# A convolution block with dynamic routing: the loop over samples written out on every engine

## The reference, cut to what matters

```python
x_proj = jnp.einsum('bchw,oc->bohw', x, proj_w)                       # 128 -> 64 channels
att1 = _route(x_proj, att1_w, att1_b, [3x3, 5x5 depthwise], 1)        # one of two kernels per sample
att2 = _route(att1, att2_w, att2_b, [7x7, 9x9, 11x11 depthwise], 3)   # one of three, dilation 3
out = jnp.concatenate([att1, att2], axis=1)
att = jnp.concatenate([out.mean(axis=1, keepdims=True), out.max(axis=1, keepdims=True)], axis=1)
att = jax.nn.sigmoid(conv7x7(att, sp_w) + sp_b)                       # two maps
gate = att[:, 0:1] + att[:, 1:2]
return out * gate + x
```

## Time and profile before

| | us |
|---|---|
| median of 3 runs | 6338.1 (6338.06 to 6348.23) |
| profiled execution, its own time | 6353.46 |
| its span | 6351.9 |
| PE busy | 4896.8 |
| DVE busy | 3135.5 |
| ACT busy | 2832.8 |
| POOL busy | 1256.7 |

### The profile page before, as it was taken

One profiled execution on the slowest core, in us unless ns is written; L12 is line 12 of the kernel. 1 busy time (PEld: TensorE's weight loads), 2 busy tenths in 40 slices (PEclk: granted clock), 3 DMA queues, 4 the chain that ended last, 5 costly groups with the idle time before them and its releaser, 6 DMA issues.

```text
span 6351.9 us, 164601 instructions
## 1 busy us (share of the span) xinstructions
PE 4896.8 (77%) x62816; PEld 3336.1 (53%) x62816; DVE 3135.5 (49%) x3835; ACT 2832.8 (45%) x5378; POOL 1256.7 (20%) x2010
## 2 busy tenths in 40 slices
PE   5678897887878788787878888787887878885453
PEld 2236464655646465564745556464555646464342
DVE  3215445464545545464554545546544554645344
ACT  3455464544545455444544545354454535452120
POOL 2001011212112121211212121121212212121332
PEclk9889898898989889798988889898798979887675
DMA  9656758869697785968779696886969688696857
GB/s 225 182 133 188 174 160 217 228 182 237 191 229 198 215 223 179 227 212 217 210 194 231 180 230 207 214 227 172 233 181 242 199 217 234 179 224 156 226 131 189
DMA packets 1015814, 1285.33 MB, mean 202 GB/s; under 512 B 670750, under 2 KB 865737, under 8 KB 984414
## 3 DMA queue, kind: packets, MB, share of 16 engines
q1 hardware_dynamic: 855500, 578.24, 39.1%
q0 software_dynamic: 90800, 555.20, 28.2%
q10 hardware_dynamic: 69026, 146.11, 8.3%
HBM read 950.16 MB, written 456.70 MB: 221 GB/s over the span
## 4 chain that ended last, share of the span: by engine, by line
PE 36%; DMA 33%; DVE 11%; issue 10%; ACT 3%; POOL 2%; SPq 2%; ACTq 1%; POOLq 0%; DVEq 0%
DMA out_dram<-RX 15%; PE psC L984 13%; DMA RX<-in_x_dram 8%; DVE MM L1198 7%; DMA RX<-w_d 5%; PE psA L922 5%; PE psA L923 5%; PE psA L858 5%; PE psB L953 3%; PE psB L867 2%; DMA RX<-nat_d 2%; PE psB L932 2%; PE psB L963 2%; DVE RX L1274 1%; DVE L L1255 1%
## 5 line engine op out<-in xcount | busy, mean ns | idle before, releaser
L984 PE MATMUL psC<-RX 61*60 61x96 f32 (+7 forms) x49152 | 1457.6, 266 | 231.6 <-POOL RX L591 96.2
L984 PEld LDWEIGHTS psC<-RX 61*60 61x60 f32 x49152 | 1391.2, 132 | 304.3 <-issue 300.1
L1198 DVE TENSOR_REDUCE MM<-L 124x135 f32<-124x6480 f32 (+3 forms) x128 | 527.6, 4194 | 587.4 <-ACT L L775 587.4
L775 ACT ACTIVATE L<-psC 124x120 f32 (+4 forms) x2048 | 393.8, 284 | 830.0 <-PE psC L984 791.2
L858 PE MATMUL psA<-RX,projt 128*64 128x512 f32 x1920 | 577.0, 686 | 236.2 <-DMA RX<-in_x_dram 162.2
L922 PE MATMUL psA<-X,RX 128*128 128x240 f32 x1280 | 642.1, 591 | 125.4 <-ACT RX L740 125.3
L953 PE MATMUL psB<-ident,L 124*128 124x124 f32 x2160 | 445.5, 356 | 347.5 <-DVE RX L1274 286.6
L591 POOL COPY RX<-RX 64x720 f32<-64x720 f32 x512 | 402.3, 792 | 1455.4 <-DMA RX<-w_d 1454.4
L745 ACT ACTIVATE X<-psA,bias 128x246 f32<-128x246 f32 x1024 | 638.4, 737 | 62.6 <-PE psA L923 46.2
L923 PE MATMUL psA<-X,RX 128*128 128x240 f32 x1280 | 632.5, 583 | 0.0
L734 ACT ACTIVATE RX<-RX 32x640 f32<-32x640 f32 x320 | 233.8, 735 | 880.7 <-PE psA L923 749.9
(11 more groups left out here) (117 smaller groups left out, 5150.9 us busy)
## 6 DMA issues: line engine op xcount, KB each, us to landing
RX<-in_x_dram POOLq DMA_DIRECT2D x64, 2560.0 KB, 11.4
RX<-w_d ACTq DMA_DIRECT2D x512, 180.0 KB, 4.4
RX<-in_x_dram SPq DMA_DIRECT2D x128, 720.0 KB, 10.6
out_dram<-RX SPq DMA_DIRECT2D x128, 720.0 KB, 14.4
nat_d<-X SPq DMA_DIRECT2D x320, 280.0 KB
RX<-nat_d POOLq DMA_DIRECT2D x208, 400.0 KB, 6.8
RX<-in_x_dram POOLq DMA_DIRECT2D x416, 200.0 KB, 5.8
out_dram<-RX POOLq DMA_DIRECT2D x416, 200.0 KB, 4.9
```

The lines of the kernel that those rows point to most:

```text
L775: ins = nc.scalar.activation(dst[:, 0:NU2 - par, 15 * r:15 * r + nq, par, :], src[:, par:BR:2, :, :], ACT.Identity)
L984: ins = nc.tensor.matmul(o[:, :, 0:kk, a:b], w2t[2 * q + p][rows, ch, z:z + PB], src[rows, 2 * p + ch, 0:nf, 3 * cg + dc:3 * cg + dc + kk, ...
L1198: nc.vector.tensor_reduce(dst[0:124, mm, :].rearrange("p (f b k) -> p f b k", f=9, k=3)[:, :, par:BR:2, :], src[:, :, 0:NU2 - par, :, par, ...
```

## The change

`samples` is changed and nothing else. All 18 turns are written out, on all five engines, each with its own copy of the turn's program. The loops inside a turn stay (`repeat` for the second convolution on PE, ACT and POOL).

```diff
         def samples(eng, body):
 
-            for s in range(4):
-                body(Turn(s))
-            with eng.Fori(4, B - 1) as s:
-                body(Turn(s))
-            for s in range(B - 1, B + 2):
+            for s in range(B + 2):
                 body(Turn(s))
```

## The result

The changed kernel takes 6274.6 us (median of 4 runs, 6264.4 to 6293.3) against 6343.2 for the kernel before on the same chip: a ratio of 0.9895, 95% interval 0.9866 to 0.9924, or 69 us less by the medians, between 48 and 85 by the interval. The forecast was 6272 us, 66 us less. Its profiled execution took 6264.4 us with a span of 6262.4.

The account below looks back on a forecast made before the run. No single engine bounds the kernel; each stage of a turn has its own last wait. Savings of 34 + 4 + 21 + 7 = 66 us, with added code at 0, took 6338.1 to 6272 us, range 6236 to 6316.

Parts of the forecast that it names:

- Step 1: Second convolution's end to projection's end: without ten branches POOL's gap before loading x block 2 goes, 3.4 us each, 34 us.
- Step 2: Routing: DVE's 30 dependent steps no longer wait for counts computed in the loop, 0.36 us a turn, 4 us.
- Step 3: First convolution with f2 and f1: looped turns come down by turn 3's 1.9 us each, 21 us.
- if the first convolution's mean doesn't move: Sign against the forecast, which expected the first convolution at 181 us on average in the profile after.
- Rival A: Whole kernel: only branches and routing count, both convolutions' differences are transfer scatter; 23 us less, 6315 us; chance 0.20.
- Step 4: Second convolution: its inner loop stays, so only a few register instructions go, 0.6 us a turn, 7 us.
- Step 5: Added code: written and looped turns run through the same straight stretches and fetch them alike; set at 0.
- rival C: Projection, f2, f1: written-out code is fetched too late for PE; two missed fetches a turn give 6353 us; chance 0.04.

Follow-up runs that it names:

- e9: Kernel before with two turns in each pass of its loop (turns 4 to 13) and turn 14 written out, on every engine; 6303.2 us, 0.9952.
- e1: Kernel before with only POOL's turns 4 to 14 written out, the other engines keeping the loop; 6292.2 us, 0.9940.
- e2: Kernel before with only PE's turns 4 to 14 written out, the other engines keeping the loop; 6314.8 us, 0.9971.
- e8: Kernel before, run unchanged for a second profile; 6324.7 us, 1.0001.
- e4: Kernel before with its loop replaced by eleven loops of one pass, whose counts were folded into constants; 6254.2 us, 0.9877.
- e6: Kernel before, loop kept on every engine, with the load of x block 2 moved ahead of the stores of map 1; 6249.5 us, 0.9891.
- e5: Changed kernel with the load of x block 2 moved ahead of the stores of map 1; 6194.9 us, 0.9793 of the kernel before.
- e7: e5 with PE turning the maps after the projection's ninth step instead of the sixth; 6126.9 us, 0.9675 of the kernel before.
- e10: e7 with the passes of the second convolution written out too; 6371.6 us, 1.0060 of the kernel before.
- e11: Changed kernel with the passes of the second convolution written out too on PE, ACT and POOL; 6499.5 us, 1.0264 of the kernel before.

## Why the prediction was right, step by step

- Step 1, branch and projection, 34 us: right in size and in cause. 3.3 us for each branch in e9, 10 branches, 33 us; POOL's 3.5 us, not PE's 3.7, is on the path (e1 against e2). One detail was wrong: what hides PE's branch is DVE's work ahead of the maps, more than the wait for block 2. Turn 3's own 64.3 us of projection, which the sum left aside, was scatter: it takes 65.4 in e8 and 66.5 in the changed kernel.
- Step 2, routing, 4 us: measured 15.64 to 15.43, 2.3 us. My reason, DVE's counts, was wrong: e2 leaves DVE in its loop and has 15.46, e1 leaves PE in it and has 15.63. It is PE's written code that shortens this stage; by which instruction stays open.
- Step 3, first convolution, 21 us: not shown. The first pair of profiles moved by 2.3 us a turn, as forecast, but the second profile of the kernel before (e8) lies at the changed kernel's value, and by the prediction's own sign ("if the first convolution's mean doesn't move") this step fails. Rival A was right on this point.
- Step 4, second convolution, 7 us: too small. 13 us come from PE's register instructions in its inner loop; the first pair of profiles shows 2.1 us a turn, 23 us.
- Step 5, code fetched in the straight part, 0: right in the sum, wrong in its reason. The queue carries less (193 packets against 218), and PE starts each turn without idle. But "fetch them alike" is not so: the "issue" stops in the second group went from 20.5 to 45.0 us, and the stage shows no cost only as PE's waits for POOL shrank by about as much. Against rival C stood that turns 0 to 3 and 15 show no such stop; turn 3 has one of 2.04 us and turn 2 one of 3.04, in the second convolution and not in the stages that C named.

The sum came out right (66 against 69) by luck in part: step 3 was put too high and step 4 too low. What the runs show, 33 + 2 + 13, is 48 us, the lower end of the measured 48 to 85; e4, nearly the same program, gave 56 to 99. Some 20 us are therefore not assigned. The first convolution averages 181.3 us over the four kernels that loop on every engine (before, e8, e6, e9) and 179.9 over the six written out on all (after, e4, e5, e7, e10, e11), which would be 15 of them, but e8 against the first profile shows that single means differ by more than that. The granted clock of this stage differs too, 0.816 on average in those four and 0.824 in those six; whether it is a cause or goes along is not shown. This stays open.

The Trainium skill's "Runtime: NRT & Kernel Launch", section "Instruction fetch mechanics", also says that kernels prefer full unrolling. For the outer loop the runs agree, with 69 us; for the inner one the measurement decides against it, 225 us slower. The Trainium skill's remark in the same section that the fetch hides behind the issue of instructions does not hold on PE in the second convolution: the changed kernel loses 45.0 us to "issue" in the second group of turns 4 to 14, and e11, where the stage is written out, stands 317 us by "issue" in all, the changed kernel 100.

## What to carry to other kernels

A loop's branch costs what the engine behind it makes late, not what that engine itself stands idle: find which engine's first act after the branch is waited for, and move that act ahead of whatever holds it, which here gave as much with the loop still in place (e6, 75 us by the medians) as removing the loop (69). Write out a long outer loop, and leave a short inner loop with back-to-back small matmuls as a loop: before writing it out, compare the bytes of its code with its time (here three packets of 16.4 KB in 11.0 us, where they came 4.9 us apart). Before sharing a gain out over stages, profile the same kernel twice; a difference between two kinds of turn inside one execution (e9) tells more than two profiles.

## What the runs showed of the hardware

- A taken branch over a turn's code costs 3.3 to 3.9 us on PE, about 6.3 on SP and about 2.8 on POOL. The branch instruction itself is recorded with 3634 ns on PE and about 50 on the other two, where the next instruction comes late.
- PE's branch over the second convolution's body, 3.0 packets of code, is recorded with 208 ns, and the changed kernel's queue carries only three packets in the whole of turn 6's second convolution; with straight code a packet of 16.4 KB came each 4.9 us there.
- Straight code of small matmuls stops PE at the packets' distance, 126 matmuls with their weight loads: in e11 all through the second convolution, and in the first pass of its loop in the kernel before and the changed one as well.
- A count from a register of the outer loop made PE's combined register instructions 85 ns instead of 37, and a steady pass of 384 matmuls 0.24 us longer.
